# The two blurs: inverse squares prepared a row of blocks further ahead, staging split between GpSimd and ScalarE, rows written out

## The reference

```python
h = relu(einsum('bchw,co->bohw', x, w1) + b1)                 # 16 channels -> 32
ks = relu(einsum('bohw,o->bhw', h, w2[:, 0]) + b2[0]) * 20.0 + 1.0
sigma = ks / 3.0
wgt = exp(-gauss_kernel / (2.0 * sigma[..., None, None] ** 2))  # 9 x 9 weights for each pixel
wgt = wgt / sum(wgt, axis=(-2, -1), keepdims=True)
low_freq = sum over u, v of xpad[u:, v:] * wgt[u, v]            # one set for all channels
enhanced = x + low_freq
result = (enhanced - mean(enhanced)) / sqrt(var(enhanced) + 1e-05)  # over h, w
```

## Time and profile before

| | us |
|---|---|
| median of 3 runs (lowest, highest) | 533.40 (532.68, 534.13) |
| the profiled execution: time | 531.34 |
| the profiled execution: span of its instructions | 529.40 |
| first blur, about | 213.7 to 345.5 |
| second blur, about | 388.3 to 529.4 |
| TensorE, VectorE, ScalarE, GpSimd busy | 412.6, 339.3, 260.6, 187.9 |

### The profile page before, as it was taken

The page is one execution under the profiler, slowest core; times in us unless marked ns, Lnnn a source line. Parts: engine busy times, 40 slices in busy tenths (PEclk is TensorE's granted clock), DMA queues, the critical chain, the costliest instruction groups (busy, mean ns, idle before and its releaser), DMA issues. The chain is left out here.

```text
span 529.4 us, 16123 instructions
## 1 busy us (share of the span) xinstructions
PE 412.6 (78%) x7024; PEld 293.8 (56%) x7024; DVE 339.3 (64%) x525; ACT 260.6 (49%) x284; POOL 187.9 (35%) x132
## 2 busy tenths in 40 slices
PE   4588998877999469668888888579956888788780
PEld 2277942225988412436666667457734666566660
DVE  2694587753888964554666668539534576566863
ACT  0664476663333000147767776511015577677771
POOL 3320013220000000307777777500030567867740
PEclk9968999996999869789999999979988899999986
DMA  8830000000000000002222223000000222222203
GB/s 190 194 136 1 2 1 0 1 0 1 4 2 1 3 0 0 1 6 79 83 84 81 80 82 84 2 1 1 0 1 0 83 85 83 84 80 80 83 4 158
DMA packets 17046, 24.67 MB, mean 47 GB/s; under 512 B 6736, under 2 KB 8545, under 8 KB 16865
## 3 DMA queue, kind: packets, MB, share of 16 engines
q1 hardware_dynamic: 15968, 23.52, 15.0%
q10 hardware_dynamic: 1024, 0.36, 0.4%
HBM read 21.53 MB, written 2.34 MB: 45 GB/s over the span
## 5 line engine op out<-in xcount | busy, mean ns | idle before, releaser
L1202 POOL TENSOR_TENSOR g_wgt<-g_exponents,g_s_wide 128x1024 f32<-128x1024 f32 x56 | 131.4, 2382 | 67.9 <-DMA g_s_wide<-g_s_rows 67.9
L1067 ACT ACTIVATE g_wgt<-g_wgt 128x2048 f32<-128x2048 f32 x64 | 121.6, 1909 | 17.2 <-DVE g_wgt L1115 11.0
L974 PE MATMUL ps<-g_wgt,g_xt 128*32 128x64 f32 x4096 | 72.5, 222 | 29.2 <-ACT g_wgt L1067 13.1
L974 PEld LDWEIGHTS ps<-g_wgt,g_xt 128*32 128x32 f32 x4096 | 62.0, 111 | 49.3 <-issue 36.9
L1115 DVE TENSOR_TENSOR g_wgt<-g_exponents,ps 128x1024 f32<-128x1024 f32 x72 | 84.6, 1202 | 2.6 <-PE ps L960 2.6
L1123 DVE COPY g_num<-ps 128x512 f32<-128x512 f32 x32 | 22.0, 687 | 64.0 <-PE ps L974 63.9
L1040 ACT ACTIVATE g_hid<-ps,vec 128x512 f32<-128x512 f32 x32 | 20.2, 683 | 84.0 <-PE ps L921 84.0
L960 PE MATMUL ps<-ident,g_scl 128*128 128x128 f32 x288 | 46.8, 302 | 4.9 <-DVE g_wgt L1115 2.6
L960 PEld LDWEIGHTS ps<-ident,g_scl 128*128 128x128 f32 x288 | 34.7, 150 | 10.4 <-DVE g_wgt L1115 4.2
L469 PE MATMUL ps<-conv_img,projblk 128*32 128x512 f32 x256 | 35.8, 679 | 0.0
L1412 PE MATMUL ps<-high,wb 128*128 128x512 f32 x72 | 30.3, 421 | 5.3 <-DVE rest L1441 5.3
(11 more groups left out here) (165 smaller groups left out, 718.0 us busy)
## 6 DMA issues: line engine op xcount, KB each, us to landing
g_s_wide<-g_s_rows SPq DMA_DIRECT2D x56, 256.0 KB, 3.8
x<-in_x SPq DMA_DIRECT2D x8, 256.0 KB, 6.8
x<-in_x SPq DMA_DIRECT2D x1, 2048.0 KB, 8.4
out<-g_result SPq DMA_DIRECT2D x4, 512.0 KB, 3.9
windows<-band SPq DMA_DIRECT2D x4, 256.0 KB, 5.1
g_s_rows<-g_srow SPq DMA_DIRECT2D x56, 4.0 KB
c_weight<-in_c_weight SPq DMA_DIRECT2D x1, 576.0 KB, 3.9
g_w<-in_g_w SPq DMA_DIRECT2D x2, 128.0 KB, 2.7
```

The costliest lines, as they stand in the source:

```text
L974: mm = pe.matmul(ps[32 * j:32 * j + 32, O_BANK, 64 * cb:64 * cb + 64], xt[(s + t) % 2][:, cb, b, :], weights_of(s, b)[:, t, cb, :], start= ...
L1067: act.activation(w, w, ACT.Exp).then_inc(weight, 1)
L1202: pool.tensor_tensor(weights_of(s, b), spread(gband[:].unsqueeze(2), shape), spread(s_wide[s][j][:].unsqueeze(1), shape), ALU.mult).then_i ...
```

## The change

- The steps of the inverse squares run one row of blocks earlier: in row r, relu, square, inverse, ks_turn and scale are those of row r+2 (before r+1), and hidden and ks those of r+3 (before r+2). They keep their places in each engine's order. The two spreads of slots 0 and 1, the exponents, the blur and the staging stay with the rows they had.
- Row 0 is a list of its own on TensorE, ScalarE and VectorE. It now holds the steps of rows 1 and 2, and hidden and ks of row 3; blur(0, half 0) stands behind ks_turn(2), and VectorE has relu(2) between its logits of images 4 and 5.
- From tile 2 on, ScalarE makes the copy of the odd blocks (`act_stage`, behind `act_xt`) and GpSimd that of the even ones; `pe_xt` waits for both.
- The hardware loop and its registers are gone: all rows are written out.
- The SyncE program is the same but for its names. What it waits for comes a row earlier.

The diff, cut to its core:

```diff
@@ -914,9 +915,12 @@
 
     def pe_hidden(pe, r):
 
-        if not is0(r):
+        if r == 1 or r == 2:
             pe.wait_ge(xt_out, r)
-        rows = bass.ds(BLK * r + R, BLK)
+        elif r > 2:
+            pe.wait_ge(xt_out, r - 1)
+            pe.wait_ge(small, 3 * r)
+        rows = slice(BLK * r + R, BLK * r + R + BLK)
...
@@ -939,7 +943,9 @@
     def pe_xt(pe, g, s):
 
         pe.wait_ge(staged, g + 1)
-        pe.wait_ge(small, 3 * RB if isinstance(g, int) and g == RB else 3 * g + 3)
+        if g >= 2:
+            pe.wait_ge(staged_a, g - 1)
+        pe.wait_ge(small, 3 * g + 3 if g < 2 else min(3 * g + 6, 3 * RB))
...
-        if do.next:
+    def pe_first_row(pe):
+
+        pe_spread(pe, 0, 0, 4)
+        pe_spread(pe, 0, 0, 5)
+        pe_ks_turn(pe, 1, 1)
+        pe_spread(pe, 0, 0, 6)
+        pe_spread(pe, 0, 0, 7)
+        pe_xt(pe, 1, 1)
+        pe_hidden(pe, 2)
+        pe_ks(pe, 2)
+        pe_spread(pe, 1, 1, 0)
+        pe_spread(pe, 1, 1, 1)
+        pe_ks_turn(pe, 2, 0)
+        pe_blur(pe, 0, 0, 0, 0)
+        pe_spread(pe, 1, 1, 2)
+        pe_hidden(pe, 3)
+        pe_blur(pe, 0, 0, 0, 1)
+        pe_spread(pe, 1, 1, 3)
+        pe_ks(pe, 3)
+
+    def pe_row(pe, r, s):
+
+        pe_blur(pe, r - 1, 1 - s, 1, 0)
+        pe_turn(pe, r - 1, 0)
+        if r + 2 < RB:
+            pe_ks_turn(pe, r + 2, s)
+        pe_blur(pe, r - 1, 1 - s, 1, 1)
+        if r + 1 < RB:
             pe_spread(pe, r + 1, 1 - s, 0)
             pe_spread(pe, r + 1, 1 - s, 1)
-        if do.main:
+        if r < RB:
             pe_xt(pe, r + 1, 1 - s)
-        if do.lag:
-            pe_turn(pe, r - 1, 1)
-        if do.main:
+        pe_turn(pe, r - 1, 1)
+        if r < RB:
             pe_blur(pe, r, s, 0, 0)
-        if do.next:
+        if r + 1 < RB:
             pe_spread(pe, r + 1, 1 - s, 2)
-        if do.after_next:
-            pe_hidden(pe, r + 2)
-        if do.main:
+        if r + 3 < RB:
+            pe_hidden(pe, r + 3)
+        if r < RB:
             pe_blur(pe, r, s, 0, 1)
-        if do.lag:
-            pe_low(pe, r - 1)
-        if do.next:
+        pe_low(pe, r - 1)
+        if r + 1 < RB:
             pe_spread(pe, r + 1, 1 - s, 3)
-        if do.after_next:
-            pe_ks(pe, r + 2)
+        if r + 3 < RB:
+            pe_ks(pe, r + 3)
 
 
...
+    def act_stage(act, g, s):
+
+        act.wait_ge(xt_mm, g - 1)
+        act.copy(*half_tile(g, s, 1)).then_inc(staged_a, 1)
+
+    def act_first_row(act):
+        act_weight(act, 0, 0, 0)
+        act_square(act, 1)
+        act_weight(act, 0, 0, 1)
+        act_xt(act, 1, 1)
+        act_stage(act, 2, 0)
+        act_hidden(act, 2)
+        act_square(act, 2)
+        act_weight(act, 0, 0, 2)
+        act_hidden(act, 3)
+        act_weight(act, 0, 0, 3)
+
+    def act_row(act, r, s):
+        if r + 2 < RB:
+            act_square(act, r + 2)
+        act_weight(act, r, s, 1)
+        act_weight(act, r, s, 0)
+        act_xt(act, r + 1, 1 - s)
+        if r + 2 <= RB:
+            act_stage(act, r + 2, s)
+        act_weight(act, r, s, 3)
+        if r + 3 < RB:
+            act_hidden(act, r + 3)
+        act_weight(act, r, s, 2)
 
 
...
@@ -1136,96 +1166,85 @@
+    def dve_first_row(dve):
+        dve_logit(dve, 0, 0, 0)
+        dve_logit(dve, 0, 0, 1)
+        dve_relu(dve, 1)
+        dve_logit(dve, 0, 0, 2)
+        dve_inverse(dve, 1, 1)
+        dve_logit(dve, 0, 0, 3)
+        dve_scale(dve, 1, 1)
+        dve_logit(dve, 0, 0, 4)
+        dve_relu(dve, 2)
+        dve_logit(dve, 0, 0, 5)
+        dve_inverse(dve, 2, 0)
+        dve_logit(dve, 0, 0, 6)
+        dve_scale(dve, 2, 0)
+        dve_logit(dve, 0, 0, 7)
+        dve_num(dve, 0, 0)
+
+    def dve_row(dve, r, s):
+        if r + 2 < RB:
+            dve_relu(dve, r + 2)
+        if r < RB:
             dve_logit(dve, r, s, 0)
-        if do.next:
-            dve_inverse(dve, r + 1, 1 - s)
-        if do.main:
+        if r + 2 < RB:
+            dve_inverse(dve, r + 2, s)
+        if r < RB:
             dve_logit(dve, r, s, 1)
-        if do.next:
-            dve_scale(dve, r + 1, 1 - s)
+        if r + 2 < RB:
+            dve_scale(dve, r + 2, s)
         dve_mix(dve, r - 1, 0)
         dve_num(dve, r - 1, 1)
-        if do.main:
+        if r < RB:
             dve_logit(dve, r, s, 2)
             dve_logit(dve, r, s, 3)
         dve_mix(dve, r - 1, 1)
-        if do.main:
+        if r < RB:
             dve_num(dve, r, 0)
         dve_enhance(dve, r - 1)
         dve_stats(dve, r - 1)
 
 
+    def half_tile(g, s, odd):
+
+        cols = pad[:, BLK * g:BLK * g + BLK, BLK * odd:BLK * odd + W]
+        return (tile[s][:].rearrange("p (k o) r c -> p o k r c", o=2)[:, odd],
+                cols.rearrange("p r (k c) -> p k r c", c=QC))
+
     def pool_stage(pool, g, s):
 
-        if not (isinstance(g, int) and g < 2):
+        if g >= 2:
             pool.wait_ge(xt_mm, g - 1)
-        for odd in range(2):
-            cols = pad[:, bass.ds(BLK * g, BLK), BLK * odd:BLK * odd + W]
-            ins = pool.tensor_copy(tile[s][:].rearrange("p (k o) r c -> p o k r c", o=2)[:, odd],
-                                   cols.rearrange("p r (k c) -> p k r c", c=QC))
-        ins.then_inc(staged, 1)
+        else:
+            pool.tensor_copy(*half_tile(g, s, 1))
+        pool.tensor_copy(*half_tile(g, s, 0)).then_inc(staged, 1)
 
...
+    def pool_row(pool, r, s):
+        for j in range(len(BY_POOL)):
+            pool_logit(pool, r, s, j)
+        if r + 2 <= RB:
             pool_stage(pool, r + 2, s)
-
-    class Row:
-
-
-
-        def __init__(self, r):
-            self.first, self.main, self.lag = r == 0, r < RB, 0 < r <= RB
-            self.next, self.after_next = r + 1 < RB, r + 2 < RB
-
-    def rows_of(eng, row):
-
-        for r in range(2):
-            row(eng, r, r, Row(r))
-        with eng.Fori(0, 2) as i:
-            for p in range(2):
-                row(eng, 2 * i + 2 + p, p, Row(2))
-        for r in range(RB - 2, RB + 1):
-            row(eng, r, r % 2, Row(r))
 
...
@@ -1262,7 +1281,9 @@
                 pool.memset(xt[s][:, :, :, C:C + 1], 1.0).then_inc(const_ready, 1)
             pool_stage(pool, 1, 1)
             pool.wait_ge(band_ready, 2)
-            rows_of(pool, pool_row)
+            pool_stage(pool, 2, 0)
+            for r in range(1, RB):
+                pool_row(pool, r, r % 2)
             if to_clear is not None:
                 pool.memset(to_clear[:], 0.0).then_inc(sem("cleared"), 1)
 
...
@@ -1279,7 +1300,9 @@
             pe_hidden(pe, 1)
             pe_ks(pe, 1)
             pe.wait_ge(const_ready, 4)
-            rows_of(pe, pe_row)
+            pe_first_row(pe)
+            for r in range(1, RB + 1):
+                pe_row(pe, r, r % 2)
 
         @block.scalar
```

More of the change, by code:

```diff
@@ L900, in is0, with image, nth @@
     def is0(r):
-        return isinstance(r, int) and r == 0
-    def slots(r):
-        return list(enumerate(range(B) if is0(r) else BY_DVE))
-    def by_slot(r, v):
-        return v + 1 if is0(r) else 4 * r + 5 + v
+        return r == 0
+    def image(r, v):
+        return v if r == 0 else BY_DVE[v]
+    def nth(r, v):
+        return v if r == 0 else B + len(BY_DVE) * (r - 1) + v
     def weights_of(s, b):
@@ L952, in pe_spread @@
             pe.wait_ge(small, 3 * r + 3)
-        if is0(r):
-            if v >= 4:
-                pe.wait_ge(logit, v - 3)
-        else:
-            pe.wait_ge(logit, 4 * r + 1 + v)
-        b = slots(r)[v][1]
+        if nth(r, v) >= 4:
+            pe.wait_ge(logit, nth(r, v) - 3)
+        b = image(r, v)
         for k in range(4):
-            tr = pe.transpose(ps[:, v % 4, P * k:P * k + P], spread(scl[s][:, k, b:b + 1], [P, P]), ident[:])
+            tr = pe.transpose(ps[:, nth(r, v) % 4, P * k:P * k + P], spread(scl[s][:, k, b:b + 1], [P, P]), ident[:])
         tr.then_inc(scl_spread, 1)
@@ L1058, in act_weight @@
     def act_weight(act, r, s, pair):
[L1060 to L1065 removed]
+        on_dve = [v for v in range(B if r == 0 else len(BY_DVE)) if image(r, v) // 2 == pair]
+        on_pool = [j for j, b in enumerate(BY_POOL) if r > 0 and b // 2 == pair]
+        if on_dve:
+            act.wait_ge(logit, nth(r, on_dve[-1]) + 1)
+        if on_pool:
+            act.wait_ge(logit_p, len(BY_POOL) * (r - 1) + on_pool[-1] + 1)
         w = wgt[s][pair][:].rearrange("p b t k m -> p (b t k m)")
         act.activation(w, w, ACT.Exp).then_inc(weight, 1)
[L1069 to L1083 removed]
+    def act_stage(act, g, s):
[24 more added lines that the diff above has]
+        act_weight(act, r, s, 2)
     def dve_relu(dve, r):
@@ L1096, in dve_inverse @@
         dve.wait_ge(ks_squared, r + 1)
-        if not (isinstance(r, int) and r < 3):
+        if not (r < 3):
             dve.wait_ge(s_stored, 64 * (r - 2))
@@ L1290, in _ @@
             act_hidden(act, 1)
-            rows_of(act, act_row)
+            act_first_row(act)
+            for r in range(1, RB):
```

(5 more changed lines are left out.)

77 lines of the change are left out of this document (12 added, 65 removed).

## The result

| | before | after |
|---|---|---|
| median, us | 533.07 (532.68 to 534.13, 4 runs) | 538.68 (536.71 to 539.81, 4 runs) |
| profiled execution: time, span | 531.34, 529.40 | 538.64, 536.41 |

The ratio is 1.0098, with a 95% interval of 1.0065 to 1.0132: the change makes the kernel 1% slower. Forecast were 529.4 us and a range of 526.0 to 533.8, so the forecast has the wrong sign. In this document a median is over all runs of a kernel, while a ratio leaves out the executions that ran in the chip's slower state, so it can differ from the quotient of two medians by half a per cent.

What follows compares the result with a forecast made beforehand. Bound: a 13.72 us row chain of TensorE, VectorE and the xt copy, without GpSimd. First blur 3.8 - 5.7 - 1.4 = -3.3, second 4.9 - 6.6 - 1.2 = -2.9, code 1.5, clock 0.7: -4.0, so 529.4 us; range 526.0 to 533.8.

Steps and rivals of the forecast that it cites:

- Code: Fetch gaps in TensorE's eight rows that become straight code: 0.2 us each, 1.5 us in all, between 0 and 10.6.
- The ring: Chain of TensorE, VectorE and xt copy steps setting a loop row's length: 3.52 + 4.37 + 1.25 + 4.58 = 13.72 us.
- What bounds a row: Rows are set by TensorE, VectorE and the xt copy; GpSimd and the DMAs are not in that chain.
- Rival 4: GpSimd's wait is the bound after all; twelve gaps of 3.2 us come back, -38, giving 495 us. Chance 0.05.
- The row in straight code: Rows written out take 13.2 us, as row 1 does, against 13.72 in the loop; other end 13.7.
- Rival 2: Loop costs nothing; the 0.51 us a row is row 1's phase. Total -0.4, 533.0 us. Chance 0.2.
- The copy on ScalarE: Half of the staging, between xt and the exp of pair 3: 0.6 us, covered by 1.87 us, cost 0.
- Rows 4 to 6: Between copies of half 0: row 4 to 5 takes 11.4 us, the next step 10.05 us.
- Row 0, chain: Serial steps for row 2 delay blur(0, half 0) by 3.3 to 4.2 us (first blur, 3.8 taken), 4.6 to 5.2 (second, 4.9).
- Row 0, clock: Thinner row 0 lowers TensorE's clock: 0.35 us for each blur, between 0 and 1.5; 0.7 us in all.
- Row 7 and the tail: GpSimd's exponents no longer hold up row 7: gain 1.4 us (first blur) and 1.2 (second); tail behind unchanged.
- rival 3: Straight code starves TensorE: gaps of 1.33 us in each row leaving the loop, 10.6 us, +5.1, 538.5 us. Chance 0.15.

Runs made afterwards that it cites:

- the first profile: Profile of one execution of the changed kernel in its first measurement, which took 538.68 us (ratio 1.0098 to the kernel before).
- the busy run: Changed kernel plus 72 identity transposes a blur, which nobody reads, wherever TensorE waits before row 1: 525.60 us (0.9877).
- the two busy runs: Unread identity transposes where TensorE waits before row 1, added to the changed kernel (525.60 us) and to the kernel before with all rows written out (523.38 us).
- the old order kept busy: Kernel before with all rows written out, plus 50 unread identity transposes where TensorE waits before row 1 of each blur: 523.38 us (0.9847).
- the run with only row 0 kept busy: Changed kernel plus 34 unread identity transposes in each blur's row 0, where TensorE waits: 535.43 us (1.0089).
- the second profile: Profile of the changed kernel run again, unchanged: 535.93 us (1.0072).

## Why the prediction was wrong, point by point

Two terms of the sum failed, both too small. Code stood at 1.5 us, and the gaps grew by 6.5. Row 0 stood at 9.4 us over the two blurs (3.8 and 4.9 for the chain, 0.7 for the clock), and it is 13.6 in the first profile and 11.1 in the second. The ring, the straight rows, and, where no gap falls, what rows 5 to 7 give back were right.

- **What bounds a row: right.** GpSimd and its DMAs are not in the ring. The changed kernel frees GpSimd of the DMAs from row 2 on, and rows 1 to 4 take the same 13.21 us as in the old order written out. Rival 4 is out. As forecast, ScalarE no longer waits for GpSimd in row 7.
- **The row in straight code: right.** 13.21 us forecast, 13.20 to 13.24 measured in the changed kernel and in the old order. Rival 2, that the loop costs nothing, is out. So is its reason, the phase of row 1: the same rows in the old order go from 13.66 to 13.21 when they are written out, 0.31 of it by the other engines' code.
- **The copy on ScalarE: right,** 0.62 us, in its cover.
- **Rows 4 to 6: right where no gap falls.** 11.4 forecast and 11.49 measured, 10.05 forecast and 10.11 in the busy run. The changed kernel had 13.01 and 10.96 in the second of them. The 13.01 has three gaps in it, 2.57 us. The 10.96 has none, but comes behind the gap of 3.08, with the clock at 0.63 from 499.5 to 502.0 us; the price of a gap goes past its own row.
- **Row 0, chain: its length right, its start and its yardstick not.** 3.3 to 4.2 and 4.6 to 5.2 forecast; between the two busy runs it is 4.5 and 6.7. From the start of xt(1) to the blur it is 7.76 us in the first blur, as summed (5.12 + 1.4 + 0.95 + 0.3), and 8.28 in the second, where the clock fell for a moment. But the forecast measured against a blur that was itself late: in the kernel before xt(1) comes 25.9 us after the first hidden matmul, in the old order kept busy 21.9 and 23.2. The new order's xt(1) comes at 19.8 and 22.7 there, so it starts 2.1 and 0.5 us earlier than the old one, and not the 3.4 and 1.9 us that the forecast reckoned with. Its chain waits for ScalarE's exp, the old one for TensorE, so a better clock gives the old order more at this place.
- **Row 0, clock: mis-sized, the first large error.** I took 0.35 us a blur, between 0 and 1.5. In the first profile row 0 is 4.9 us over the chain that I had summed, for the 0.7 of both blurs; in the second it is 2.4 over. Against the run with only row 0 kept busy it is 3.5 and 3.2 us, with 0.7 as the least in the other profiles. I had the row that shows a clock of 0.50 and priced one spread or one blur part at it. But the price is that of everything on the serial chain while the clock is low: hidden(2) +1.8 us from xt to relu, the first blur part and its spread +0.9. And I asked only what the new idle time adds, not what the old one already cost.
- **Code: mis-sized, the second, and the largest.** I took 1.5 us of new gaps, 0.2 for each row that becomes straight, from the three gaps in the straight rows of before. Measured are 9.95 us for 3.47, 6.5 more. What failed is the step from "straight rows beside the same reads have run clean" to the other rows: where a gap falls is fixed by the code, so eight old rows say little on eight new ones, and its length hangs on the reads. From the copy of row 1 to that of row 6 it is 65.2 and 65.7 us for the 61.1 forecast. Of the Trainium skill's rule (Runtime: NRT & Kernel Launch, section Instruction fetch mechanics), that the cost of a block boundary is mostly hidden, the trace without reads in the old order shows the same (no gap); the traces with reads don't, and neither does that of the new order without reads (5.28 us).
- **Row 7 and the tail:** 1.4 and 1.2 us forecast, 1.24 and 2.29 measured, with gaps of 1.6 us in the first blur that belong to code.

The sum was -3.3 and -2.9 with 2.2 us for code and clock; the profiles have +3.5 and +5.5. The forecast of rival 3 was 538.5, and the time is 538.68, but only half for its reason: it had 10.6 us of gaps in the rows that left the loop and row 0 as forecast. The gaps are there, in size, but they are also in rows 6 and 7, and row 0 was 4.2 us dearer than forecast, which a cheaper row 7 and 2.0 us less outside the blurs hide.

How the loss divides, from the runs. With the transposes the new order costs 2.6 us in the blurs (257.4 for 254.8). Without them it is 4.8 (267.8 in the second profile, for 262.9 in the old order written out), so 2.2 more. These are not in row 0: the transposes shorten the way to the first copies by 6.7 us over both blurs in the new order (34.64 and 39.60 to 32.04 and 35.49) and by 6.9 in the old one. They are in the gaps, which fall from 9.91 to 5.61 us in the new order and from 6.63 to 6.36 in the old; why 72 more instructions do this wasn't tested, but they move all later places in the code. The first profile has 2.5 us more than the second in row 0, by its clock; this part is luck from execution to execution. Writing the rows out changes nothing that can be told from noise (0.9982, 0.9940 to 1.0024).

What stays open: why the new order has gaps without a read before them (5.0 us in the run without the reads) and the old one, written out, has none. I argued that rows 5 to 7 of the new order are the fastest, 9.3 to 11.5 us, so TensorE needs its next block sooner. That wasn't tested, and it can't be all, since the old order without the reads has a step of 9.26 us as well and no gap.

## What to carry to other kernels

A wait in the profile is worth removing if somebody waits for the engine that waits: some 40 us of the 67.9 here, all but the two waits of some 13.7 us each in the first rows, held up nearly nobody: ScalarE waited for GpSimd twice, 6.1 us. Where an engine's work comes early in a serial start, price the clock over the whole chain, and try filling TensorE's idle time with matmuls that nobody reads; with 50 transposes a blur the old order went from 530.31 to 523.38 us, with 72 the new one from 535.93 to 525.60, both clear of the noise (4.3 us of the second are fewer gaps). And before unrolling a loop on TensorE, look at what else is on the DMA engines when it crosses from one block of code to the next: issuing the same four reads in twos took the gaps from 6.4 to 0.5 us here, and the time from 523.38 to 520.31 us, which by itself is within the noise.

## What the runs showed of the hardware that I had not expected

- TensorE stops in the middle of equal matmuls, up to 3.14 us, and goes on 2.2 to 2.8 us after a packet of 16 KB of instructions. The place is fixed by the code (eight of nine gaps behind the same matmul in two profiles of the same kernel), the length depends on the reads (at one matmul 3.08 and 2.80 us with them, 1.16 without). In the old order four reads of 256 KB a row in one burst go with 6.36 us of gaps, two and two with 0.52, none with 0; in the new order 5.28 us are left without reads.
- A handover in a row of the loop, with what is waited for and the addresses in registers, took 0.08 to 0.21 us longer than in a row written out; over the three engines of the ring 0.45 us a row (13.66 to 13.21).
- A long gap has a tail, and it is the clock: after 3.14 us of standing still TensorE worked for 4.9 us at a granted clock of 0.50, four transposes took 1.12 us for 0.66, and the row lost 0.7 us beyond the gap.
- The same row 0 runs at different clocks from one execution to the next: 34.64 and 37.15 us to the first copy in two profiles of the same kernel.
